# Gelu of an expert's eight hidden blocks in one ScalarE visit instead of two

## The reference, cut to what matters

```
o  = softmax(q k^T / sqrt(hd)) v @ wo + x          # 32 heads
xe = o.reshape(MB=2, E=8, tpe, D)                   # rows of each expert by position
h  = gelu(einsum(metd,edf->metf, xe, w1) + b1)      # D=256 -> 1024
y  = einsum(metf,efd->metd, h, w2) + b2             # 1024 -> 256
```

## Time and profile before

| | |
|---|---|
| median of 3 runs | 1309.32 us (1307.38 to 1309.88) |
| span of the profiled execution, first to last instruction | 1303.5 us |
| PE busy | 1085.2 us (83%) |
| DVE busy | 750.8 us (58%) |
| ACT busy | 481.6 us (37%) |
| the main loop | from about 110 to 950 us |
| the mixture | from there to the end |

### The profile page before, as it was taken

The page is one execution under the profiler, slowest core; times in us unless marked ns, Lnnn a source line. Parts: engine busy times, 40 slices in busy tenths (PEclk is TensorE's granted clock), DMA queues, the critical chain, the costliest instruction groups (busy, mean ns, idle before and its releaser), DMA issues. The chain is left out here.

```text
span 1303.5 us, 23306 instructions
## 1 busy us (share of the span) xinstructions
PE 1085.2 (83%) x8482; PEld 775.5 (59%) x8482; DVE 750.8 (58%) x2013; ACT 481.6 (37%) x970; POOL 211.7 (16%) x248
## 2 busy tenths in 40 slices
PE   1228997987999898889988889897898999999990
PEld 1224664544666356666455553584547999999980
DVE  7982445675555857748677466355453444545445
ACT  2111332445465444346533555251202333333332
POOL 3960000000000000200001100000223333333320
PEclk7557998989999889899987899698899999999995
DMA  5023141009521479022805130020960111111105
GB/s 168 18 51 140 50 175 38 18 17 179 66 74 65 192 209 106 33 67 73 162 1 73 58 106 1 1 65 11 372 233 29 38 38 38 38 38 37 38 30 197
DMA packets 73422, 108.90 MB, mean 84 GB/s; under 512 B 16593, under 2 KB 58337, under 8 KB 72865
## 3 DMA queue, kind: packets, MB, share of 16 engines
q1 hardware_dynamic: 66192, 74.75, 23.2%
q0 software_dynamic: 5280, 14.57, 3.4%
q10 hardware_dynamic: 1840, 18.10, 3.3%
HBM read 83.47 MB, written 40.97 MB: 95 GB/s over the span
## 5 line engine op out<-in xcount | busy, mean ns | idle before, releaser
L1688 DVE TENSOR_REDUCE mx<-scores_ps 128x4 f32<-128x1024 f32 (+1 forms) x160 | 186.9, 1168 | 86.6 <-PE scores_ps L1163 46.5
L1516 ACT ACTIVATE pt<-turned_ps 128x1024 f32<-128x1024 f32 (+1 forms) x160 | 158.0, 987 | 151.8 <-PE turned_ps L1159 103.8
L2224 PEld LDWEIGHTS x_ps<-x_xtT,x_w1s 128*128 128x128 f32 x1248 | 145.3, 192 | 3.4 <-ACT x_xtT L2252 1.5
L2224 PE MATMUL x_ps<-x_xtT,x_w1s 128*128 128x128 f32 x1248 | 145.8, 275 | 1.1 <-ACT x_xtT L2252 1.1
L2238 PE MATMUL x_ps<-x_experts,x_hT 128*128 x624 | 141.0, 379 | 0.0
L2238 PEld LDWEIGHTS x_ps<-x_experts,x_hT 128*128 128x128 f32 x624 | 115.6, 190 | 14.1
L1056 POOL COPY vpad<-v 128x64 f32<-128x64 f32 x64 | 13.4, 240 | 638.6 <-PE ps L1198 526.5
L1149 PE MATMUL turned_ps<-q,k 32*128 32x256 f32 x512 | 70.4, 351 | 28.5 <-DVE mx L1688 19.3
L1149 PEld LDWEIGHTS turned_ps<-q,k 32*128 32x128 f32 x512 | 42.9, 200 | 82.9 <-issue 43.3
L2267 ACT ACTIVATE x_hT<-x_ps,x_b1c 128x128 f32<-128x128 f32 x312 | 84.9, 382 | 16.9 <-issue 13.8
L2287 DVE COPY x_w1s<-x_experts 128x2048 f32 x39 | 55.9, 1435 | 49.0 <-PE x_ps L2224 37.4
(11 more groups left out here) (430 smaller groups left out, 2007.6 us busy)
## 6 DMA issues: line engine op xcount, KB each, us to landing
x_slots<-x_slots ACTq DMA_DIRECT2D x4, 4160.0 KB
wexp<-in_L_ffn_w SPq DMA_DIRECT2D x16, 1024.0 KB, 5.5
x_experts<-in_L_ffn_W SPq DMA_DIRECT2D x16, 1024.0 KB, 13.8
q<-heads SPq DMA_DIRECT2D x48, 128.0 KB, 5.4
k<-heads SPq DMA_DIRECT2D x48, 128.0 KB, 10.3
ha<-h SPq DMA_DIRECT2D x16, 256.0 KB, 3.2
x_pair<-y_rows SPq DMA_DIRECT2D x4, 1024.0 KB, 9.2
heads<-nat_k_hi SPq DMA_DIRECT2D x12, 256.0 KB, 4.2
```

What stands on the lines that cost most here:

```text
L1516: sc.activation(pt[v.index // 2 % (PT_RING // 2)][:, :, 0:wide], turned_ps[:, :, 0:wide], ACT.Exp)\
L1688: v.tensor_reduce(mx[:, u.group % 2, 0:blocks, u.n:u.n + 2].rearrange("p b n -> p n b"), scores_ps[:, :, 0:blocks * (P if u.causal else T) ...
L2224: last = mm(ps[2 * (i % 2) + f // KH][:, f % KH * P:(f % KH + 1) * P], w1s[:, i % 2, c, f * P:(f + 1) * P], xtT[:, i % 2, c, :], start=c = ...
```

## The change

The plan's table gives the visits of ACT another place and another length: none at the slot `up{e}1`, 5.2 instead of 3.2 at the slot `up{e}3`. ACT's code for the stage applies Gelu to all eight blocks of an expert when it reaches n = 3. The Gelus themselves, their number and their operands stay.

```diff
@@ class Plan, STAGES["Y1a"]
-                [(1.75, .7, 0, True, f"up{e}0"), (1.75, .7, 3.2, False, f"up{e}1"), (1.75, .7, 0, False, f"up{e}2"),
-                 (1.75, .7, 3.2, False, f"up{e}3"), (.9, 0, 0, True, f"down{e}0+1"), (.9, 1, 0, False, ""),
+                [(1.75, .7, 0, True, f"up{e}0"), (1.75, .7, 0, False, f"up{e}1"), (1.75, .7, 0, False, f"up{e}2"),
+                 (1.75, .7, 5.2, False, f"up{e}3"), (.9, 0, 0, True, f"down{e}0+1"), (.9, 1, 0, False, ""),
@@ scalar engine, y1a
-                    if n % 2:
-                        for m in (n - 1, n):
+                    if n == 3:
+                        for m in range(4):
                             added(act, f"up{e}{m}", p)
                             for i in range(2):
                                 f = 2 * m + i
```

## The result

The changed kernel takes 1319.17 us (median of 4 runs, 1316.7 to 1320.45), the kernel before on the same chip 1308.96 us (4 runs, 1307.38 to 1309.88). The ratio is 1.0063, with a 95% interval from 1.0034 to 1.0091: slower. The forecast had this side and put it at +2.5 us; it was about +10. The profiled run took 1319.09 us with a span of 1317.0, 13.5 us more than the span of before. In this run, and in every run of the experiments, time and span differ by 2.0 to 2.2 us. The kernel before, measured again beside the experiments (77 runs), ranged from 1301.3 to 1318.4: a difference of one trace against one trace counts for little by itself.

A forecast was written before the change was run, and what follows sets the result against it. PE bounds pair 2's feed-forward, instruction order the loop's end. Terms -1.2 + 0.5 + 0.5 + 2.7 - 8.0 + 8.0 + 0 = +2.5 us took 1309.3 to 1311.8; own range 1308 to 1316, 8 in 10 within 1301 to 1321.

The forecast's parts named there:

- Table loads: On ACT, two of four visits per pair go: 20.5 us less of ACT, not on the path.
- Pair 1's wait: PE's wait of 3.17 us ahead of pair 1's first down products shrinks to 2.0: gain 1.2 us.
- Pair 0's new wait: Pair 0's longer ACT visit is just about covered by PE work: 0.5 us of new wait, 0 to 1.3.
- Pair 2's feed-forward part: Two more attention slots where PE has no hole cost 2.7 us; new waits of pair 2's two visits 0.5.
- The end of the attention: The stretch 808.6 to 817.8, with waits between its PE work, goes: -8.0 us, between 5.55 and 9.20 gained.
- Pair 3 up to the last down product: Moved work, state scaling, norm wait and lower clock make this stretch 8.0 us longer, between 0.9 and 10.
- the wait for `g_o`: Pair 2's norm steps now follow the second expert's fourth eviction: PE idle 3.4 us ahead of the `ob` transposes.
- The scaling of the state: DVE's 2.47 us step now stands ahead of pair 3's first up evictions: 2.5 us longer, 0 to 3.
- Behind it: After pair 3's last down product, earlier transposes gain 5.8, given back by gate work: 0, between -3.2 and +3.3.
- Rival A: The new order pays, PE's waits in pair 3 don't appear: about -5.5 us, 1303.8; chance 0.28.
- Rival C: Waits at `g_o` and the thinner chain behind it lower the clock more often: +8 more, about 1320; chance 0.12.
- The third sign of being wrong: A half-clock stretch appears or vanishes in pairs 0 to 2, which the sum took as unchanged.

The follow-up runs named there:

- e1: Kernel before with only ScalarE's code changed to one visit of eight Gelus per expert, order of before kept: 1310.41 us, ratio 0.9998.
- e2: Changed kernel's order on every engine, but ScalarE's two visits of four Gelus as in the kernel before: 1327.75 us, ratio 1.0129.
- e4: One visit; order of before up to pair 2's third up product, the changed kernel's from there on: 1322.58 us, ratio 1.0091.
- e7: Changed kernel with pair 2's last two gate slots moved behind pair 3's third value product and q projection: 1319.2 us, ratio 1.0081.
- e9: One visit; order of before, except the changed kernel's from slot 344 up to and with pair 2's state: 1315.96 us, ratio 1.0031.
- e3: One visit; changed kernel's order up to pair 2's third up product, the order of before from there on: 1310.91 us, ratio 1.0001.
- e8: One visit, order of before, but pair 3's fillers and first transposes ahead of pair 2's gate product: 1302.73 us, ratio 0.9954 to the kernel before.
- e10: One visit; order of before up to the third up product of pair 3's first expert, then the changed kernel's: 1314.03 us, ratio 1.0029.
- e5: Changed kernel with two more filler products in each of the last eight attention slots, 16 in all: 1322.46 us, ratio 1.0099 to the kernel before.
- e11: e8 with the added filler products of e5 in the attention slots from 169 on: 1312.88 us, ratio 1.0025 to the kernel before.
- e6: Changed kernel with pair 2's last two norm steps on VectorE ahead of the second expert's up evictions: 1325.56 us, ratio 1.0111.

## Why the forecast had the side and missed the size

The forecast of 1311.8 named its own range as 1308 to 1316, and 1319.2 is above it. That the side came right is in part luck: two large terms were both missed, by 6.2 and by 7.8 us, and cancel for the most part; what is left over is the 5.8 us behind them that the sum put at 0.

- *Table loads.* Right for ACT: 20.5 us less. Off the path nothing came in the old order. The rule to group by table set (the Trainium skill, "ScalarE: Activation LUTs", "Rules for kernel authors") gave its 20.5 us of ACT in every kernel with one visit. It gave no time in the old order (e1) and 5 to 8 us in the new one (e2); PE's waits for `pt` at L1149 are 10.6 us in all in e2's trace and 7.8 in the changed kernel's, which is less than that.
- *Pair 1's wait.* 2.0 forecast, 1.52 us measured ahead of its first down products, in place of 3.17. Right.
- *Pair 0's new wait.* 0.5 forecast, 0 to 1.3; 1.41 us measured ahead of its first down products (373.99), where none was. A little over.
- *Pair 2's feed-forward part.* 2.7 for two slots and 0.5 for waits; measured 3.5, of them 43.84 - 41.60 = 2.2 busy. Right.
- *The end of the attention.* -8.0 forecast, first transposes at 828.1. Measured 825.87, just outside the 826 to 831 that the forecast had set for itself, although pair 2 began 3.0 us later than in the trace of before. From pair 2's last down product to these transposes it is -14.2: more than the stretch of 9.20 us that I let go could give. In the traces 9.5 us of it are busy time and 4.7 idle time, in front of that stretch as well: the clock over the whole of it is 0.88 in place of 0.81, and two slots are gone. The waits for `mx` (2.1 us in this part before) are gone too, but those for `pt` grew from 1.1 to 2.9. The kernels with this order (e2, e4 to e7, e9) show -12.8 to -14.3, those with the old one and no fillers (e1, e3, e8, e10) -0.5 to +1.5. Mis-sized.
- *Pair 3 up to the last down product.* 8.0 forecast, 15.8 measured. This is the step that failed. Of its parts the moved work (3.2 + 0.7 against 2.85) and the wait for `g_o` (3.26 against 3.4) are right, and so is the half projection (1.9 against 2.0). The scaling of the state did not hold up the products behind it: in the trace after no wait for L1940 is left. In its place there are waits of 0.6 to 0.9 us between the short products, 4.1 in the rows above from L1275 to L1425 (before, 0.80 and 0.72 stood in this part), and 1.48 at the second expert. And the clock was priced at 1.3. Measured: L1275 6.60 against 4.0 us for the same 16 products, L1358 15.6 against 14.4, L1370 16.1 against 14.4, the transposes of `yb_b` 1.9 against 1.3: 6.1 us. I had seen that the first stretch of half clock becomes shorter in the new order, and took from it that it would cost less. It starts at about the same time (817.9) and lasts until 835, as before until 838. But what runs in it has changed: the attention slots end 8 us earlier in it, and the whole of a projection that PE does without a hole, of which before only the start stood there, takes their place. And after a short return to the full clock it falls again from 839 to 848, behind the score products with their holes.
- *Behind it.* 0 forecast, between -3.2 and +3.3. Measured -1.0 + 5.6 + 1.2 = +5.8. The transposes came at 11.3 us as forecast (11); then the clock took 1.85 us at them (3.93 against 2 x 1.04) and 3.0 at the value products (8.42 against 5.42), and gave back 1.6 at the gate product (1.95 against 3.55). The gate steps inside the chain are worth 3.7 us by e7, close to the +3.3; that the clock comes on top is what I left out.
- *Rival A* (faster) was to decide at `g_o`: PE waited for it, so it fell. *Rival C* (the clock falls more often, 1320) gave the number that came, and has a good part of the cause: half clock from 839 to 848, and for two thirds of 901 to 919 (PEclk 0.66 to 0.68), where before a shorter piece stood earlier, at the gate product and the fillers. But it expected the falls behind the wait at `g_o` and in the chain that follows. Around that wait (858.6 to 879.0) the clock is 1.00 and behind it, to 890, 0.85; the largest fall, from 839 on, it did not name. That its number is so close is in part luck. It had 0.12, for the reason just told, and that reason was the error. The mechanism of the forecast, new waits in pair 3, is there too; e9 and e10 show 6.7 and 3.9 us for the two places in their traces (4.5 and 2.6 in the medians), and in the first of them, by the one trace of e5, about 4.4 are clock.
- *Sums and signs.* The lower end of all terms together is -11.8, not -11; the terms for pair 3 up to the last down product add up to 8.6 at their upper ends, not 10; and the 5.8 us that the median stands above the span of before are 2.1 around the span, the rest what executions differ by. The third sign of being wrong, a stretch of half clock that appears in pairs 0 to 2, came true in the trace: from 530 to 546 the clock is 0.57 in place of 0.83. It is no effect of the order, since e3, with the same order there, lacks it. The sum had no room for such spread.

Open: where the single visit's 5 to 8 us lie in the new order (e2), why e5's runs without a trace are 10 us slower than the one with it, and why in e11 the clock is low at 903 to 914 when fillers run ahead of 840; the trace shows the two together and no more. Also that a gain at the z product comes back in part by the mixture (e7, e8) has no cause here that I could point to.

## What to carry to other kernels

Where a build-time table sets the order, a change of its numbers is a change of the kernel of its own: measure the code with the old order first (e1: 0), then each half of the new order (e3: 0, e4: all of the loss). Where one kernel's runs spread over 17 us, as here, read a part's cost from landmarks inside the trace and from several traces, not from one span. When work moves behind the end of a busy phase, price it at the clock that its new neighbourhood has in the trace, and ask which full products will stand inside the slow stretch. Moving a step up DVE's queue did not mend the wait for it: the wait went to what stands behind it there (e6).

## What was not expected of the hardware

In this trace the Gelu table is loaded when the instruction comes up, not when its data do. In pair 3's second expert it runs at 859.88, and then ACT waits 9.38 us for the first eviction, so this load costs no time:

```profile
859.88 1.28 ACT L1591 ACT_TABLE_LOAD   x1
870.53 1.70 ACT L1591 ACTIVATE hid<-hid,b1c 128x256 f32<-128x256 f32 x4 [9.38 <-DVE hid L1870]
```

The granted clock does not follow PE's work at once: in e9 it was 0.56 over 10 us in which PE was busy throughout, behind 30 us in which it was busy for 23.2. And sixteen products of 0.45 us (ten take 4.46), added for the clock's sake in e11, went with a low clock at another place and about 9 us more in the median. Whether one caused the other is not shown.
